# Relative attention: each pair of exponentials before the copy of transposed weights, in ScalarE's order of work

## What is computed

```
def _L1_xattn_ref(query, key, value, ...):
    q = query @ Wq + bq;  k = key @ Wk + bk;  v = value @ Wv + bv
    ...
    attn1 = jnp.einsum('bhqd,bhkd->bhqk', rq, rk)
    rel_k = rel_k_table[_rel_idx(t, s)]
    attn2 = jnp.einsum('bhqd,qkd->bhqk', rq, rel_k)
    attn = jax.nn.softmax((attn1 + attn2) / scale, axis=-1)
    w1 = jnp.einsum('bhqk,bhkd->bhqd', attn, rv)
    rel_v = rel_v_table[_rel_idx(t, s)]
    w2 = jnp.einsum('bhqk,qkd->bhqd', attn, rel_v)
    x = (w1 + w2).transpose(0, 2, 1, 3).reshape(b, t, D_MODEL)
    return x @ Wo + bo
```

## Time and profile before

| what | value |
|---|---|
| median of 3 runs | 3100.84 us (3099.18 to 3106.6) |
| the profiled execution, its own time | 3077.52 us |
| its span | 3075.8 us |
| mean granted clock of TensorE | 0.894 of full speed |
| TensorE busy, weight loads busy | 79%, 63% of the span |
| VectorE, ScalarE, GpSimd busy | 51%, 41%, 21% of the span |

### The profile page before, as it was taken

How to read it: one execution, slowest core, us unless ns; L and a number is a source line. 1 busy time by engine, 2 the same in 40 slices (tenths; PEclk the granted TensorE clock), 3 DMA queues, 4 the chain that set the end, 5 groups by cost and what they waited for, 6 DMA issues and landing times. The chain is left out here.

```text
span 3075.8 us, 55876 instructions
## 1 busy us (share of the span) xinstructions
PE 2435.5 (79%) x19120; PEld 1931.1 (63%) x19120; DVE 1562.0 (51%) x2968; ACT 1251.9 (41%) x2768; POOL 648.2 (21%) x722
## 2 busy tenths in 40 slices
PE   5968999994639999975996799999999998594046
PEld 3647888883629999964775466666666666352034
DVE  3663555553701111116996365666556665645764
ACT  1211222221013434323664355555555554446750
POOL 1000111111754444333443111111111111000000
PEclk8998999995569999996997899999999998697578
DMA  3012212116119999972001655555555553110211
GB/s 88 22 32 52 58 48 58 48 48 205 51 60 341 343 345 342 344 217 63 0 0 27 128 120 123 117 119 118 123 118 115 122 117 69 47 80 32 80 48 43
DMA packets 389949, 346.86 MB, mean 113 GB/s; under 512 B 73572, under 2 KB 368254, under 8 KB 387838
## 3 DMA queue, kind: packets, MB, share of 16 engines
q1 hardware_dynamic: 374526, 329.16, 37.9%
q0 software_dynamic: 15360, 16.88, 2.6%
HBM read 258.78 MB, written 87.20 MB: 112 GB/s over the span
## 5 line engine op out<-in xcount | busy, mean ns | idle before, releaser
L1919 ACT COPY rel_probT<-rel_ps_t 121x400 f32<-121x400 f32 x384 | 196.3, 511 | 248.6 <-PE rel_ps_t L2136 248.6
L2136 PE MATMUL rel_ps_t<-rel_ident,rel_prob 100*121 100x100 f32 x1536 | 249.6, 286 | 35.3 <-ACT rel_probT L1919 35.2
L2136 PEld LDWEIGHTS rel_ps_t<-rel_ident,rel_prob 100*121 100x121 f32 x1536 | 197.3, 187 | 111.9 <-ACT rel_probT L1919 82.6
L1931 ACT ACTIVATE rel_prob<-rel_ps_s,rel_nmx 100x361 f32<-100x361 f32 x512 | 264.3, 579 | 2.9 <-DVE rel_nmx L2020 2.9
L1092 PEld LDWEIGHTS moe_ps_h<-moe_xeT,moe_w 128*128 128x128 f32 x2048 | 240.2, 193 | 5.1 <-issue 1.9
L1092 PE MATMUL moe_ps_h<-moe_xeT,moe_w 128*128 128x128 f32 x2048 | 240.8, 276 | 1.3 <-DVE moe_xeT L1259 1.3
L2020 DVE TENSOR_REDUCE rel_nmx<-rel_ps_s 100x2 f32<-100x722 f32 x256 | 232.8, 909 | 8.8
L1092 PE MATMUL moe_ps_y<-moe_w,moe_hT 128*128 128x256 f32 x1024 | 231.4, 379 | 0.0
L2613 PE MATMUL ffd_ps_y<-ffn_w_dT,ffd_oq 128*100 128x256 f32 x384 | 86.1, 388 | 162.1 <-DVE ffd_oq L2589 162.1
L1092 PEld LDWEIGHTS moe_ps_y<-moe_w,moe_hT 128*128 128x128 f32 x1024 | 189.6, 190 | 23.2
L1083 ACT ACTIVATE moe_hT<-moe_ps_h,moe_b 128x128 f32<-128x128 f32 x512 | 142.5, 375 | 140.8 <-PE moe_ps_h L1092 140.4
(11 more groups left out here) (423 smaller groups left out, 5301.1 us busy)
## 6 DMA issues: line engine op xcount, KB each, us to landing
moe_w<-in_L_ffn_w SPq DMA_DIRECT2D x128, 1024.0 KB, 9.7
rel_scores<-rel_r_ext SPq DMA_DIRECT2D x32, 818.8 KB
rel_r_key<-rel_scores SPq DMA_DIRECT2D x32, 818.8 KB
rel_weights<-rel_prob SPq DMA_DIRECT2D x128, 204.7 KB
rel_by_dist<-rel_weights SPq DMA_DIRECT2D x32, 400.0 KB
mut_ctx_nat<-in_ctx SPq DMA_DIRECT2D x32, 363.0 KB
mut_ctx_T<-in_ctxT SPq DMA_DIRECT2D x32, 361.0 KB
rel_ctx_T<-in_ctxT SPq DMA_DIRECT2D x32, 361.0 KB, 4.4
```

Source lines behind the costliest of these rows:

```text
L1919: nc.scalar.copy(probT[:, pg % 2, c], ps_pT).then_inc(s_t_sb, 1)
L1931: last = nc.scalar.activation(prob[:, t.parity, slot, :], ps_s[0:S, j, 0:L], ACT.Exp, bias=nmx[:, slot:slot + 1])
L2136: last = nc.tensor.transpose(ps_pT[:, j, :], prob[:, pt.parity, QUAD * pg + j, c * STEP:c * STEP + R], ident[0:S, 0:S])
```

## The change

In ScalarE's list for a group, the first pair of exponentials now precedes the first copy of transposed weights, and the second pair precedes the second copy. Before, each pair followed that copy. The jobs stay in their places between them. Nothing is added or removed, and the lists of the other engines are not touched.

```
@@ -1937,11 +1937,11 @@
                 for g in range(GROUPS):
                     pt, pg = group(t, g)
                     empty(t, 4 * g)
+                    weights(t, g, 0)
                     transposed(pt, pg, 0)
-                    weights(t, g, 0)
                     empty(t, 4 * g + 1)
+                    weights(t, g, 1)
                     transposed(pt, pg, 1)
-                    weights(t, g, 1)
                     empty(t, 4 * g + 2)
                     transposed(pt, pg, 2)
                     empty(t, 4 * g + 3)
```

## The result

| | before | changed |
|---|---|---|
| median of ten runs | 3101.84 us (3094.9 to 3106.6) | 3114.91 us (3106.39 to 3118.95) |
| ratio, 95% interval | | 1.0040 (1.0029 to 1.0052) |
| profiled execution, its span | 3077.52, 3075.8 us | 3113.42, 3111.7 us |

Slower by 13 us, or 0.4%, where 19.7 us were forecast. The time lies in the forecast range of 3110 to 3139 us, in its lower part.

What follows compares the result with a forecast made beforehand. TensorE, 92% busy in a ping-pong with ScalarE's copies, was taken as the bound. Group terms +25.1 - 7.0 + 1.6 = +19.7 us on the 3100.84 median gave 3120.5 us, range 3110 to 3139.

Steps and rivals of the forecast that it cites:

- Group 0, the loss: Group 0: second copy 0.81 us later, all passed on to group 1's scores; 31 turns, +25.1 us.
- the step that failed: Side effects: weights leave up to 1.3 us sooner; transfers and GpSimd's masking serve later groups, with no TensorE wait shown.
- Group 1, the gain: Group 1: second exponentials finish sooner, so group 2's scores start 0.22 us earlier; 32 turns, -7.0 us.
- Group 2: Group 2: first copy slips 0.04 us behind the first pair; taken as 0.05 over 32 turns, +1.6 us.
- Group 3: Group 3: first pair disappears into 3.36 us of ScalarE idle time before the first copy; no change either way.
- The sum: Whole stage: +25.1 - 7.0 + 1.6 = +19.7 us, 0.64 us a turn; bounds +15 to +33.
- The delay is absorbed: Rival: a later TensorE wait shrinks by group 0's 0.8 us delay, leaving only group 1's gain; 3093.8 us, chance 0.12.
- The clock: Rival: TensorE's clock drops to its lower level for one group a turn; 64 us more, 3184, chance 0.03.
- The late maximum: Rival: ScalarE stands at late maxima while transposes lie ready; 8 us more, 3128, chance 0.04.

Runs made afterwards that it cites:

- experiment 3: Kernel before with ScalarE's new order in group 0 only, the other groups in the old order; 3125.78 us, ratio 1.0072.
- experiment 2: Kernel before with ScalarE's new order in group 3 only; 3086.86 us, ratio 0.9959.
- experiment 8: Changed kernel with GpSimd's mask also waiting until VectorE emptied the previous turn's last job, so it starts just ahead of L2027; 3190.94 us, ratio 1.0297 to kernel before.
- experiment 6: Changed kernel with VectorE normalising a later turn's rows (L2027) before emptying group 3's last job; 3097.3 us, ratio 0.9993 to kernel before.
- experiment 7: Kernel before, ScalarE's order unchanged, with VectorE normalising a later turn's rows (L2027) before emptying group 3's last job; 3082.03 us, ratio 0.9947.
- 10: Kernel before with rows normalised (L2027) before group 3's last job is emptied and ScalarE's new order in group 3 alone; 3061.94 us, ratio 0.9877.

## Why the prediction was right, and where it was not

**Group 0, the loss: right in mechanism and size.** "The second copy 0.81 us late" was tested by itself in experiment 3: 0.77 us. In the changed kernel the second copy starts 5.87 us after the scores, which is the forecast 6.28 less the 0.39 that came back, to 0.02.

**Group 0, the step that failed.** The prediction said of the new times of GpSimd's masking that they "work for later groups, which no row shows TensorE waiting for. If they had been needed, that would be a gain". Its result was not needed sooner, but the time in which it runs was. GpSimd's mask had been holding L2027, on TensorE's path, for 0.39 us a turn in 28 turns; 28 x 0.39 = 11 us came back. The trace of before showed it, had L2027's 0.79 us been set beside the 0.40 and 0.41 us of the two executions that nothing held. The prediction had named its own sign for this: "I am wrong if the period of group 0 grows by less than 0.7". It grew by 0.39.

**Group 1, the gain:** 0.17 measured, 0.22 forecast. **Group 2:** 0.02 and 0.05. **Group 3:** nothing on TensorE, as said; its effects were on when GpSimd's mask runs and, with the rows early, on the wait for a transfer.

**The sum.** With the missing term it would have been 19.7 - 28 x 0.39 = 8.8 us, a time of 3109.6 us. The 13 measured lie above, since the ends of the loop lose more than forecast: group 0 of turns 1, 30 and 31 lost 3.7 us together, where the sum has 3 x 0.81 = 2.4 for them, and some 3 us more lie in other groups there. Part of that is chance: group 1 of the last turn took 6.87 and 4.91 us in the two profiles of the kernel before. The prediction had no term for the ends, only 3 us of range, and those on the side of a shorter time. The two errors have opposite signs, so the total looks better than its working, and that the time lies inside the range is in part luck.

**The rivals.** "The delay is absorbed" came nearest to what happened: a wait of TensorE shrank by half the delay. But it shrank in front of the delay, not behind it, and by itself: experiment 2 has the gain with no delay. The clock did not fall in the changed kernel, where TensorE waits 0.7 and 0.4 us; experiment 8 shows the price at 2.36 us of standing. The late maximum cost time in experiment 6 alone.

## What to carry to other kernels

Before moving work on one engine, list what its results release on the others, and ask not only who needs them sooner but what runs beside them at the old and at the new time. An instruction of one shape whose duration has two values may be held by something: look at what the neighbour engine does until its end. When a reordering has parts, try each place by itself: here one of four groups held all of the loss, and the other three were worth 13 us.

## What the runs showed of the hardware

VectorE's normalisation of rows (a tensor_scalar that reads and writes SBUF) does not finish while GpSimd's mask (a tensor_tensor with both inputs in SBUF) runs: it ended 0.15 us behind the mask whether it started 0.64 us (kernel before) or 1.89 us (experiment 8) before the mask's end. Ahead of turn 1 of the changed kernel the mask's row starts 0.04 us behind the normalisation's, and that one too ended 0.15 us behind the mask. The hold stands in the profile as a longer duration, 0.79, 2.04 or 2.49 for 0.40 us, and as no wait. At the start of the stage in the kernel before, GpSimd's spreading of the queries (0.85 and 0.86 us) held it in the same way, twice, to 0.92 and 0.93 us and an end 0.15 us behind. VectorE's addition from PSUM (0.42 us) and its statistics (0.43 us) ran wholly beside the mask 31 times in the kernel before and took the same time as without it.

The Trainium skill, SBUF — State Buffer, section Who interferes with whom, has this as a rule: VectorE and GpSimd share one pair of ports, which one instruction locks for its whole length; tensor_scalar can need that pair, in a mode that uses two ports and if its operands allow it; and an instruction with at most one input in SBUF, outside those modes, does not contend. The trace agrees: the tensor_scalar was held until the mask ended, the addition and the statistics were not.

Open: why, with the rows early and ScalarE's order of before, the wait for the weights by distance is three times as long (experiment 7). Open too: VectorE's first maxima of a turn end 0.2 to 0.3 us later after the scores in every other turn of each kernel here in which nothing holds L2027, the changed kernel and experiments 6, 7 and 10 among them. A row of such a turn, experiment 6, has 0.20 us before the addition, put to the engine itself ("issue") and not to another:

```profile
2098.94 0.44 DVE L2017 TENSOR_TENSOR rel_ps_s<-rel_ps_s,rel_r_key 100x262 f32<-100x262 f32 x1 [0.20 <-issue]
```

The kernel's loops (`turns`) run two turns per pass, and the late turns are 5, 7, and so on to 27, which are those that follow VectorE's jump back to the start of its loop. The jump is thus the likely cause, but no run tests it.
